# Small expert tiles: one 256-column product for high weights times both activation halves, the two partial sums added by VectorE

## The reference

```
gate_weights = jax.nn.softmax(einsum('bsd,dn->bsn', x, Wg) + bg)
topv, topi = jax.lax.top_k(gate_weights, 2)
h = gelu(einsum('bsd,ndh->nbsh', x, W1) + b1)     # 256 -> 512
h = gelu(einsum('nbsh,nhf->nbsf', h, W2) + b2)    # 512 -> 512
eo = einsum('nbsf,nfd->nbsd', h, W3) + b3         # 512 -> 256
out = sum over the two chosen experts of eo * topv
```

## Time and profile before

| what | value |
|---|---|
| median of 3 runs (lowest to highest) | 732.91 us (731.61 to 738.06) |
| the profiled execution's own time | 732.86 us |
| its span | 731.0 us |
| mean granted TensorE clock | 0.899 of full speed |
| busy: PE, DVE, ACT, POOL | 561.6, 433.2, 299.7, 254.8 us |
| tile loop of the experts | about 205 to 354 us |
| steps from one single's layer 2 to the next | about 8.5 us |

### The profile page before, as it was taken

One profiled execution on the slowest core, in us unless ns is written; L12 is line 12 of the kernel. 1 busy time (PEld: TensorE's weight loads), 2 busy tenths in 40 slices (PEclk: granted clock), 3 DMA queues, 4 the chain that ended last, 5 costly groups with the idle time before them and its releaser, 6 DMA issues.

```text
span 731.0 us, 12063 instructions
## 1 busy us (share of the span) xinstructions
PE 561.6 (77%) x4143; PEld 396.7 (54%) x4143; DVE 433.2 (59%) x994; ACT 299.7 (41%) x742; POOL 254.8 (35%) x297
## 2 busy tenths in 40 slices
PE   3948799167289999999977989889888467764765
PEld 2537344155169989777634647566576245543333
DVE  3586899955645554444474553535555656767674
ACT  1511200243533443433343744816564355545553
POOL 3950478845600000000378863917612200010000
PEclk9979899755689999999999999999999789996796
DMA  8592310555641111110230000000000500000000
GB/s 289 183 370 92 127 58 0 172 163 183 205 171 59 34 56 45 38 31 23 59 108 0 1 1 1 1 0 1 1 1 1 172 1 3 2 2 0 7 22 30
DMA packets 32248, 49.62 MB, mean 68 GB/s; under 512 B 3096, under 2 KB 22368, under 8 KB 31808
## 3 DMA queue, kind: packets, MB, share of 16 engines
q1 hardware_dynamic: 29888, 41.65, 17.1%
q0 software_dynamic: 2304, 7.21, 2.8%
HBM read 39.68 MB, written 9.18 MB: 67 GB/s over the span
## 4 chain that ended last, share of the span: by engine, by line
PE 50%; POOL 15%; DVE 15%; ACT 11%; issue 4%; DMA 3%; SPq 0%; ACTq 0%; DVEq 0%; POOLq 0%
PE bank L1559 15%; PE bank L1574 4%; PE bank L1722 4%; POOL sm L523 3%; POOL rq L516 3%; POOL sorted_rows L498 3%; POOL qs L518 2%; POOL rq L514 2%; ACT pT L818 2%; PE bank L1437 2%; PE bank L1967 2%; DVE xn L924 2%; PE bank L1866 2%; PE bank L1466 1%; PE bank L1468 1%
## 5 line engine op out<-in xcount | busy, mean ns | idle before, releaser
L666 ACT ACTIVATE hf<-bank,be 128x256 f32<-128x256 f32 (+1 forms) x120 | 44.3, 420 | 75.3 <-PE bank L1559 59.1
L1559 PE MATMUL bank<-h,wsp 128*128 128x256 f16 (+1 forms) x720 | 72.5, 250 | 2.6 <-DVE h L1117 1.4
L504 POOL DMA_INDIRECT yg<-expert_rows,pos x16 | 15.8, 989 | 164.9 <-DMA expert_rows<-yb 160.3
L1559 PEld LDWEIGHTS bank<-h,wsp 128*128 x720 | 60.6, 97 | 13.7 <-issue 4.8
L1115 DVE CAST h<-hf 128x512 f16<-128x512 f32 (+1 forms) x60 | 21.9, 365 | 64.0 <-ACT hf L666 63.1
L486 POOL TENSOR_TENSOR kvp<-xnT,cxT 128x512 f32<-128x512 f32 x32 | 35.6, 1135 | 43.2 <-issue 33.3
L721 ACT ACTIVATE sm<-sm,nm 128x128 f32<-128x128 f32 x128 | 49.8, 393 | 1.0 <-DVE nm L1230 1.0
L576 ACT CAST wsp<-wraw 128x2048 f16<-128x2048 f32 x12 | 22.7, 1900 | 65.8 <-DMA wraw<-in_L_ffn_W 65.8
L464 POOL TENSOR_TENSOR wsp<-wraw,wsp 128x512 f16<-128x512 f32 x40 | 45.8, 1177 | 9.1 <-ACT wsp L576 8.8
L1227 DVE SCALAR_TENSOR_TENSOR sm<-bank,const 128x512 f32<-128x512 f32 x32 | 22.1, 691 | 38.6 <-PE bank L1689 38.6
L523 POOL TENSOR_TENSOR sm<-sm,rinv 128x512 f32<-128x512 f32 x32 | 33.1, 1040 | 24.3 <-DVE rinv L1221 24.3
(11 more groups left out here) (299 smaller groups left out, 1314.7 us busy)
## 6 DMA issues: line engine op xcount, KB each, us to landing
wraw<-in_L_ffn_W SPq DMA_DIRECT2D x16, 512.0 KB, 5.2
wraw<-in_L_ffn_W SPq DMA_DIRECT2D x8, 1024.0 KB, 5.9
cxT<-in_ctxT SPq DMA_DIRECT2D x2, 1024.0 KB, 7.5
tap<-in_taps SPq DMA_DIRECT2D x1, 2048.0 KB, 14.3
xg<-sorted_rows SPq DMA_DIRECT2D x8, 256.0 KB, 3.1
expert_rows<-yb SPq DMA_DIRECT2D x8, 256.0 KB, 2.2
sorted_rows<-early POOLq DMA_DIRECT2D x1, 1536.0 KB, 12.0
sorted_rows<-early POOLq DMA_DIRECT2D x1, 1408.0 KB, 15.3
```

Source lines behind the costliest of these rows:

```text
L666: last = nc.scalar.activation(hf[:, p, n * k:n * k + n], bank[2 * (layer - 1) + p][:, n * k:n * k + n], ACT.Gelu, bias=be[:, layer - 1, u, ...
L1559: last = nc.tensor.matmul(b[:, n * (f % 2):n * (f % 2) + n], w[a_][:, c, P * f:P * f + P], inp[:, b_, c, :], start=(c == 0 and a_ + b_ == ...
```

## The change

Only tiles of 128 rows change, in layers 1 and 2. For each chunk the high weights are now multiplied with both activation halves at once, as one product of 256 columns (128 high, 128 low), and the low weights with the high half, 128 columns, into the first half of the same columns. So each chunk has two products in place of three, with two weight loads in place of three. High-times-low now stands in PSUM columns of its own: a block f takes 256 columns of its bank in place of 128. VectorE adds the two column halves with a `tensor_reduce` over an axis of length 2, one for each bank, and writes the sum, 128x256 fp32, to a free half of `hf` in SBUF. ACT's Gelu waits for that (semaphore `halves_added`) and reads SBUF in place of PSUM. In VectorE's order both additions of a layer stand ahead of the layer's first cast.

```diff
@@ hidden (ACT)
                 for p in range(2):
-                    act.wait_ge(sem(f"l{layer}_psum"), 2 * j + p + 1)
+                    if n == P:
+                        act.wait_ge(sem("halves_added"), 4 * (j - PAIRS) + 2 * layer + p - 1)
+                        sums = hf[:, p, SLOTS:2 * SLOTS]
+                    else:
+                        act.wait_ge(sem(f"l{layer}_psum"), 2 * j + p + 1)
+                        sums = bank[2 * (layer - 1) + p]
...
-                        last = nc.scalar.activation(hf[:, p, n * k:n * k + n], bank[2 * (layer - 1) + p][:, n * k:n * k + n],
+                        last = nc.scalar.activation(hf[:, p, n * k:n * k + n], sums[:, n * k:n * k + n],
@@ split_hidden (DVE)
                 h = packed((h1 if layer == 1 else h2)[:], n)
+                if n == P:
+                    for p in range(2):
+                        dve.wait_ge(sem(f"l{layer}_psum"), 2 * j + p + 1)
+                        if layer == 1 and j == PAIRS:
+                            dve.wait_ge(sem("h2_lo"), 2 * j + p - 1 + CREDIT)
+                        halves = bank[2 * (layer - 1) + p][:].rearrange("p (f a n) -> p f n a", f=2, a=2)
+                        nc.vector.tensor_reduce(hf[:, p, SLOTS:2 * SLOTS].rearrange("p (f n) -> p f n", f=2), halves, AX.X, ALU.add).then_inc(sem("halves_added"), 1)
@@ layer (PE)
+                            if n == P:
+                                both = b[:, 2 * n * (f % 2):2 * n * (f % 2) + 2 * n]
+                                nc.tensor.matmul(both.rearrange("p (a n) -> p a n", a=2), w[0][:, c, P * f:P * f + P], inp[:, :, c, :], start=(c == 0), stop=False)
+                                last = nc.tensor.matmul(both[:, 0:n], w[1][:, c, P * f:P * f + P], inp[:, 0, c, :], start=False, stop=(c == chunks - 1))
+                                continue
                             for a_, b_ in passes:
```

## The result

The changed kernel takes 738.63 us in the median of 20 runs, the kernel before 734.35 in as many: a ratio of 1.0054 with a 95% interval of 1.0036 to 1.0073, 2.6 to 5.4 us more (the ratio is worked out from all runs; the two medians alone would give 1.0058). 736.4 and +3.5 us had been forecast.

What follows compares the result with a forecast made beforehand. PE's sequencer, with two register steps a chunk, was taken to bound the singles, so fewer products save nothing. The longer chain through DVE adds 1.25 + 0.7 + 0.8 + 0.73 = +3.5 us: 736.4 us, range 731.0 to 741.0.

Steps and rivals of the forecast that it cites:

- The products are free: Layers 1 and 2 of singles: two register steps pace a chunk, about 273 ns, so removing the third product saves nothing.
- The sum at 0.68 us: Each new VectorE reduction, from 512 fp32 PSUM columns to 256 in SBUF, was costed at 0.68 us.
- Rival C: Sums on VectorE are dear, 1.07 us a reduction: total +11.7, 744.6 us; chance 0.11.
- rival D: Sums on VectorE are cheap (0.425 us) or hidden anyway, so rounds cost nothing: 733.6 us; chance 0.07.
- The sum of 3.5 us: Whole kernel: first single, five rounds, last single and its tail together lengthen the time by 3.5 us, to 736.4.
- first single: Tile 8: layer 2's third chunk waits for the second half's subtraction, so layer 2 ends at 301.06, not 300.35: +0.7 us.
- five rounds: Layer 2 of tile 8 to that of tile 13: the longer DVE chain adds 0.25 us a round, +1.25 us.
- last round: Tile 13 to layer 2 of tile 14: third chunk starts 5.04 us after layer 1's first product, not 4.24: +0.8.
- tail: Last single's layer 3: the second half's first product stands 2.32 us after layer 2's end, not 1.59: +0.73.
- Gelu from SBUF: ScalarE's two Gelus of a bank stay at 0.62 us; 30 ns per Gelu would move the chain by 0.12 us.
- Nothing behind the loop changes: The stretch after 354 us should only be shifted by 3 to 4 us, with no change of length foreseen.
- Rival B: Products pace the singles: a chunk falls from 273 to 202 ns, sum -2.9, 730.0 us; chance 0.10.

Runs made afterwards that it cites:

- two_nosum: Kernel before with the changed two products a chunk but no sums on VectorE, high weights times low activations left out: 733.17 us, ratio 0.9972.
- three_sums: Changed kernel with the 256-column product split again into two of 128 columns in chunks c > 0, sums kept: 739.44 us, ratio 1.0064.
- three_regs: Kernel before with three register instructions a chunk in place of two in the singles, same products: 761.01 us, ratio 1.0361.
- copy_half: Changed kernel with a cheaper copy of the first column half in place of each sum: 734.63 us, ratio 0.9989.
- the static pair: Kernel before and changed kernel, each with fixed experts and no register instructions on TensorE: 712.14 and 726.91 us.
- static_after: Changed kernel with fixed experts, so no register instructions on TensorE: 726.91 us, ratio 0.989 against the kernel before.
- static_before: Kernel before with fixed experts, so no register instructions on TensorE: 712.14 us, ratio 0.969.

## Why the prediction was right, and where it was off

**The products are free: right.** In the changed kernel's layer 2 of tile 9 the loads start one by one, 0.12 us apart (timeline of the weight loads):

```profile
304.23 0.10 PEld L1572 LDWEIGHTS bank<-h,wsp 128*128 x1
...
304.35 0.10 PEld L1573 LDWEIGHTS bank<-h,wsp 128*128 x1
...
304.48 0.10 PEld L1572 LDWEIGHTS bank<-h,wsp 128*128 x1
...
304.60 0.10 PEld L1573 LDWEIGHTS bank<-h,wsp 128*128 x1
```

That is the step of the earlier trace rows, with the group of two gone. Layers 1 and 2 of the next single (tile 10) take 6.65 us together (2.34 from 307.91, 4.31 from 312.56), near the 6.6 that the prediction named as a sign. two_nosum, three_sums and three_regs say the same from three sides. Of the 0 to 0.1 us a tile that I left open for fewer instructions, at most 0.07 is there.

**The sum at 0.68 us: right.** 0.688. Rival C and rival D both hung on this price; copy_half shows D's mechanism at work with 0.423: the rounds cost nothing, while the first and the last single cost 1.8 us where D had 0.74.

**The sum of 3.5 us: right in kind, 1.5 us short in the loop.** The terms, each with what it measured in the profiled execution:

| term | predicted | measured |
|---|---|---|
| first single, layer 1 to the end of layer 2 | +0.7 | 9.05 against 8.20: +0.85 |
| five rounds | +1.25 | 44.90 against 42.73: +2.17 |
| last round | +0.8 | 8.91 against 7.78: +1.13 |
| tail, to the copy of the last tile | +0.73 | 3.24 against 2.45: +0.79 |
| sum | +3.48 | +4.94 |

The interval of the times, 2.6 to 5.4 us, holds both sums, so only the trace tells them apart. The term that was mis-sized is "Gelu from SBUF", which left the pair at 0.62 us. Read from SBUF a Gelu takes 392 ns and not 363, and the pair 0.69 us (308.67 to 309.36 in the round above). Two pairs lie on the chain of a round: +0.14; the prediction had said that 30 ns a Gelu would move it by 0.12, and had left that out of the sum. Counted from the first product of layer 1 (E = 307.91 in the round shown), the third chunk of layer 2 starts at 313.11, so 5.20 us after E where I had 5.04; before it was 4.79. That is +0.41 a round in place of +0.25, and puts the rounds at 8.97, just above the 8.7 to 8.9 that I had named as a sign. The five rounds carry 0.92 of the missing 1.46 us.

One hand-over was mis-sized too. What stands on the chain ahead of layer 2 is the first half's subtraction: it ends at 312.32, and the first chunk starts 0.24 us later, where I had taken 0.15 for such a hand-over. Two chunks at PE's pace lead from there to 313.11. The second half, which I had as the last wait, is there almost as late (timeline of DVE):

```profile
312.55 0.42 DVE L1129 TENSOR_TENSOR h<-hf,h 128x256 f16<-128x256 f32 x1
```

It ends 0.14 us ahead of the third chunk. The two ways to 313.11 end together, and this trace does not tell which of them holds it.

Of the rest, 0.15 lies in the first single, 0.33 in the last round and 0.06 in the tail. In the last round the third chunk starts 5.17 us after E (343.92 to 349.09), 0.13 later than I had it; the other part is pace. Before, PE had instructions in hand there: layer 2 of tile 14 took 4.08 us and that of tile 9 4.37. The changed kernel waits ahead of layer 2 and loses that lead (4.29 us, 348.54 to 352.83), which the prediction did not count.

**Nothing behind the loop changes: not contradicted.** From the last copy to the end the kernel before takes 377.7 us and the changed one 376.9; over the other kernels this stretch is 374.9 to 382.6, so a change of one microsecond there can't be seen in one profile.

**Rival B was wrong in its premise and in its gain.** Products do not pace these singles, and where they do, in the static pair, a chunk gains 2 ns and not the 71 of B's sum. What B's sum had right is that the chain through DVE binds then: static_after loses to static_before.

## What to carry to other kernels

Before products are merged, look at what stands between them in the sequencer: here two register instructions a chunk, 0.124 us each, hid a third of the products completely, and of the edits tried here only those that took such instructions out of the loop paid. A product that is off the pace is worth next to nothing, while the addition that replaces it goes onto the path of another engine in full; so weigh such a trade in the round of each engine, from the last product to the next layer's first. A step that only looks late in an engine's order may lie under a wait that is there anyway, and undoing it then gives nothing.

## What I had not expected of the hardware

- A Gelu of 128x128 takes 392 ns from SBUF and 363 from PSUM; also in three_sums (392) and two_nosum (364, from PSUM). The Trainium skill ("VectorE: DVE Perf Modes", Specifications) says that ScalarE sits closer to PSUM. These traces agree: the difference is about 29 ns an instruction.
- With a register instruction at the head, the first chunk of layer 2 starts 0.24 us after the first half's subtraction (312.32 to 312.56); with a fixed address 0.15 (305.30 to 305.45 in static_after). In the last tile's layer 3 the second half's product starts 0.15 us after its subtraction with register addresses and 0.06 with fixed ones (334.51 to 334.57 in static_before). So in both places a register address costs about 0.1 us at the wait too, not only in the stream.
- Moving one register load out of the round saved 0.67 us, three times what the profile shows as issue ahead of layer 2: the sequencer's lead over the array counts as well (18 products in the first 1.04 us of layer 2 in place of 13).
- With three register instructions a chunk, the lower clock of the array cost nothing: 48 products took 6.38 us with 3 us of them at a granted clock of 0.50, and 6.38 at 1.00 (three_regs).
